# First attention: causal masks added by one full-array bf16 product per head, in place of four over half arrays

## The chip, the cores and the metric

One core of one Trainium2 chip (trn2). The metric is the device time of one execution in microseconds; less is better. The kernel is written in a language that names every instruction, its engine and its semaphores, so nothing is reordered by a compiler: each engine runs its own list in the order in which the source issues it.

## What is computed

The whole is a two-block transformer on x of shape (8, 512, 256): attention with rope, a mixture of 8 experts, a second attention with its MLP, and a mixture of 64 experts. The change touches the first attention only, 16 heads of 16 dimensions over 8 sequences of 512 tokens:

```python
att = jnp.einsum('bhtd,bhsd->bhts', q, k) * (1.0 / math.sqrt(DH))
causal = jnp.tril(jnp.ones((t, t), dtype=bool))
att = jnp.where(causal, att, -jnp.inf)
att = jax.nn.softmax(att, axis=-1)
y = jnp.einsum('bhts,bhsd->bhtd', att, v)
```

## The kernel before

`attention0_phase` works sequence by sequence (8 of them) and, inside one, head pair by head pair (8 pairs, r = 0 to 7). A pair has its two heads j = 0, 1 stacked: head 0 lives in rows (partitions) 0 to 63 of `kq_T`, head 1 in rows 64 to 127. Score products are taken over 64 rows each, the one of head 0 in the upper half of TensorE's array and the one of head 1 in the lower half, and write two different PSUM banks of a ring tile (`banks(k)[:, j, ...]`). q and k carry a high and a low part side by side, which is why 64 rows are used for 16 dimensions.

Each pair is scored twice. The steps a0, a1, a2 (L665 to L679) compute scores with tokens in rows, from which VectorE takes each token's maximum (L468). The maximum is negated and written into the q stack (L474, L477), which step m transposes again (L662). The steps b0, b1, b2 (L681 to L692) compute the transposed scores with the maximum already subtracted, and ScalarE exponentiates them into `probs` (L532). Steps v0 to v3 (L704) multiply them with the values into `pO`, once for two pairs; these products use 32 columns of the array. Step h copies `pO` out on ScalarE (L541), step o transposes it (L712), and VectorE divides (L485, L487). Only blocks on and below the diagonal are computed, one tile of 128 rows by 512, 384, 256 or 128 columns per block row: a0 and b0 hold the one of 512 columns, a1 and b1 those of 384 and 128, a2 and b2 the one of 256. That is 8 tiles per pair, 64 per sequence, 512 in all, and each is done for two heads.

Every tile crosses the diagonal in one 128x128 block, and there the mask is added by TensorE itself, as a product of an identity with a triangle of -1e30 into the same PSUM accumulation. Before the change this product too is taken in halves: the 128 rows of the identity and the triangle are cut into two parts u = 0, 1 of 64 rows, each part is kept twice (in the upper and in the lower half of the partitions), and each head adds both parts from its own half of the array: four products per tile (L676 for a, L690 for b), all in fp32r. Of the two parts one is all zero over half of its columns, so it takes 64 columns and the other 128.

The order of TensorE's work is written out by hand. `STEP` gives the order within a step and how far ahead of the current pair each kind runs, and `BETWEEN` puts the work of neighbouring sequences between: x (transposes of the next sequence's input, L558), p0 to p3 (its qkv projections, L551), t and y (transposes, L577, and projection of the last sequence's attention output). Those, the transposes qk (L656), m and o all use the whole array of 128 rows by 128 columns:

```python
STEP = (("qk", 3), ("a0", 2), ("b0", 0), ("v0", -1), ("m", 1), ("a1", 2), ("b1", 0), ("v1", -1), ("a2", 2),
        ("v2", -1), ("b2", 0), ("v3", -1), ("h", -1), ("o", -1))
BETWEEN = {("qk", 0): ("x",), ("a0", 0): ("p0",), ("a1", 0): ("p1",), ("a0", 1): ("p2",), ("a1", 1): ("p3",),
           ("b1", 0): ("t",), ("b1", 1): ("y",)}
```

v, h and o exist for odd r only. A step with an even pair behind it is called even in this text: it has no v, h, o. The first sequence has no t and y, the last no x and p. Three ring tiles of two PSUM banks go round through qk, a, b, x, p, t and y; a unit may begin when the unit three places earlier has been taken by its reader (`wait_taken`). VectorE and ScalarE run through the same ORDER. GpSimd prepares the next sequence's stacks (L220 to L236).

At the start SP issues the loads one after another on one queue: x of the first sequence, weights, biases and rope, x of the next, then the constants into the unused `probs[2]`, then the third part of x, then stores of zeros to DRAM (L281). VectorE rounds the constants (`constants()`, L377 to L384) between the first bias additions and its share of the first stacks. TensorE's `prepare` ends with waits for the constants, and its first `body` with a wait for the stacks.

Of the kernel before, what the change touches and what calls it, by code (L numbers as in the profile page):

```python
# [24 lines left out]
F32R = mybir.dt.float32r  # L25
BF16 = mybir.dt.bfloat16
# [6 lines left out]
P = 128  # L33
# [55 lines left out]
def attention0_phase(nc, g, t):  # L89

    W3 = 3 * D
    with ExitStack() as ctx:
        def sb(name, shape, dt=F32):
            return ctx.enter_context(nc.sbuf_tensor("a0_" + name, shape, dt))
# [12 lines left out]
        rope = sb("rope", [P, TB, 2, DH0])  # L107
        unrope = sb("unrope", [P, TB, 2, DH0])
        HALF = P // 2
        half_eye = sb("half_eye", [P, 2, P], F32R)  # L110
        mask_ts = sb("mask_ts", [P, 2, P], F32R)
        mask_st = sb("mask_st", [P, 2, P], F32R)
        ident_r = sb("ident_r", [P, P], F32R)

        stats, mv = sb("stats", [P, NT, 6]), sb("mv", [P, NT, 2])
# [25 lines left out]

        w_raw = probs[0][:, :, :].rearrange("p j c -> p (j c)")[:, 0:KC * W3].rearrange("p (c n) -> p c n", c=KC)
        wp_raw = probs[1][:, 0, 0:KC * D].rearrange("p (c n) -> p c n", c=KC)
        const_raw = probs[2][:, 0, 0:6 * P].rearrange("p (m u q) -> p m u q", m=3, u=2)

        ring = [ps(f"ring{k}", (P, 2 * S)) for k in range(3)]
        pT = ps("pT")
# [96 lines left out]
        @block.sync  # L244
        def _(sp):
            x_in = t["x"].rearrange("b (n p) d -> p (b n) d", p=P)

            def load_x(batch):
                a, b = BATCHES[batch]
                sp.dma_start(g.x[:, a:b, :], x_in[:, a:b, :]).then_inc(x_loaded[batch].sem, x_loaded[batch].tick(16))  # L250

            load_x(0)
            for dst, src in (
                (w_raw, t["wqkv"].rearrange("(c p) n -> p c n", p=P)),
                (g.ident[:, :], t["ident"][:, :]),
                (wp_raw, t["wproj"].rearrange("(c p) n -> p c n", p=P)),
            ):
                sp.dma_start(dst, src).then_inc(loaded.sem, loaded.tick(16))
            for dst, src in (
                (bias_qkv[:, :], t["bqkv"].partition_broadcast(P)),  # L260
                (unrope[:, :, :, :], t["unrope"].rearrange("(n p) q d -> p n q d", p=P)),
                (rope[:, :, :, :], t["rope"].rearrange("(n p) q d -> p n q d", p=P)),
                (bias_proj[:, :], t["bproj"].partition_broadcast(P)),
            ):
                sp.dma_start(dst, src).then_inc(rest_loaded.sem, rest_loaded.tick(16))
            load_x(1)
            for j in range(2):
                rows = slice(j * HALF, (j + 1) * HALF)
                for u in range(2):
                    cut = slice(u * HALF, (u + 1) * HALF)  # L270
                    sp.dma_start(const_raw[rows, 0, u, :], t["ident"][cut, :]).then_inc(const_loaded.sem, const_loaded.tick(16))
                    for kind in range(2):
                        sp.dma_start(const_raw[rows, 1 + kind, u, :], t["causal"][kind, cut, :]).then_inc(const_loaded.sem,
                                const_loaded.tick(16))
            load_x(2)

            sp.wait_ge(zeros_ready.sem, zeros_ready.at(1))
            zeros = heads_T[:, :].rearrange("p (n d) -> p n d", d=D)
            step = zeros.shape[1] * P
            for at in range(0, TOKENS, step):  # L280
                sp.dma_start(t["sorted_x"][at:at + step, :].rearrange("(n p) d -> p n d", p=P), zeros).then_inc(zeroed.sem,  # L281
                        zeroed.tick(16))
            sp.wait_ge(zeroed.sem, zeroed.at(zeroed.n))
            for rows, start in (("sorted_x", TOKENS), ("sorted_y", 0)):
                for at in range(start, BLOCKS * SLOT_TOKENS, TOKENS):
                    size = min(TOKENS, BLOCKS * SLOT_TOKENS - at)
                    dst, src = (t[name][a:a + size, :].rearrange("(p r) d -> p (r d)", p=P)
                                for name, a in ((rows, at), ("sorted_x", 0)))
                    sp.dma_start(dst, src).then_inc(spread_zeros.sem, spread_zeros.tick(16))
            sp.wait_ge(spread_zeros.sem, spread_zeros.at(spread_zeros.n))  # L290
# [46 lines left out]
        def _(dve):  # L337
# [38 lines left out]
            def constants():  # L376
                dve.tensor_tensor(wp_lo[:, :, :], wp_raw, wp_hi[:, :, :], ALU.subtract).then_inc(w_split.sem, w_split.tick())  # L377
                assert w_split.n == SPLITS
                dve.tensor_copy(ident_r[:, :], g.ident[:, :]).then_inc(const_split.sem, const_split.tick())
                dve.wait_ge(const_loaded.sem, const_loaded.at(12 * 16))  # L380
                for ins in (
                    dve.tensor_copy(half_eye[:, :, :], const_raw[:, 0]),
                    dve.tensor_copy(mask_ts[:, :, :], const_raw[:, 1]),
                    dve.tensor_copy(mask_st[:, :, :], const_raw[:, 2]),  # L384
                ):
                    ins.then_inc(const_split.sem, const_split.tick())

# [158 lines left out]
        def _(pe):  # L546
# [75 lines left out]
            def body(s, m, before, more):  # L622
                pe.wait_ge(stacked.sem, stacked.at(2 * TB, s))
                absent = (() if before else ("t", "y")) + (() if more else ("x", "p"))
                for what, r in ORDER:
                    if what in absent:
                        continue
                    if (what, r) in PLACE:
                        u = PLACE[what, r]
# [35 lines left out]
                    elif what in ("a0", "a1", "a2"):  # L665
                        pe.wait_ge(evac.sem, evac.at(r + 1, s))
                        for tb, at in A_TILES[int(what[1])]:
                            diag = at + tb * P
                            for j in range(2):
                                rows = slice(j * HALF, (j + 1) * HALF)  # L670
                                pe.matmul(banks(k)[:, j, at:at + (tb + 1) * P], kq_T[rows, q_at(r), tb * P:(tb + 1) * P],
                                          kq_T[rows, k_at(r), 0:(tb + 1) * P], start=True, stop=False)
                            for u, cut in ((0, slice(0, P)), (1, slice(HALF, P))):
                                for j in range(2):
                                    rows = slice(j * HALF, (j + 1) * HALF)
                                    last = pe.matmul(banks(k)[:, j, diag + cut.start:diag + cut.stop], half_eye[rows, u, :],  # L676
                                                     mask_ts[rows, u, cut], start=False, stop=(u == 1))
                        last.then_inc(scores.sem, scores.tick())
                    elif what in ("b0", "b1", "b2"):  # L679
                        if what == "b0":  # L680
                            pe.wait_ge(max_evac.sem, max_evac.at(r + 1, s))  # L681
                        for sblk, at in B_TILES[int(what[1])]:
                            for j in range(2):
                                rows = slice(j * HALF, (j + 1) * HALF)
                                pe.matmul(banks(k)[:, j, at:at + S - sblk * P], kq_T[rows, k_at(r), sblk * P:(sblk + 1) * P],
                                          qT_max[r % 2][rows, sblk * P:S], start=True, stop=False)
                            for u, cut in ((0, slice(0, HALF)), (1, slice(0, P))):
                                for j in range(2):
                                    rows = slice(j * HALF, (j + 1) * HALF)
                                    last = pe.matmul(banks(k)[:, j, at + cut.start:at + cut.stop], half_eye[rows, u, :],  # L690
                                                     mask_st[rows, u, cut], start=False, stop=(u == 1))
                        last.then_inc(shifted.sem, shifted.tick())  # L692
                    elif what in ("v0", "v1", "v2", "v3"):
                        group, sblk = r // 2, int(what[1])
# [1923 lines left out]
```

## Time and profile before

| | |
|---|---|
| median of 3 runs | 2916.57 us (2913.05 to 2918.31) |
| profiled execution, span from first to last instruction | 2917.1 us |
| first attention, from TensorE's first scores to its last | about 54 to 672 us |
| TensorE / VectorE / ScalarE / GpSimd busy over the span | 85% / 63% / 46% / 28% |
| mean granted clock of TensorE | 0.926 |

The page gives no time for the profiled execution beside its span; the span lies within the runs. "PE" is TensorE's products, "PEld" its weight loads, "DVE" VectorE, "ACT" ScalarE, "POOL" GpSimd, "SP" the sync engine. In a product `out<-a,b`, b is the stationary operand that is loaded first. A shape such as 64*128 is the part of the array that is used, rows by columns; 64x384 behind it is what is streamed. Two instructions on the two halves of the array start 2 to 4 ns apart, so the timeline merges them (x2, x4). The end of a product is modelled, so what counts is the distance between starts. The recorded start of a product is never later than the end of its load, but it may be earlier than the time at which it streams.

### The profile page before, as it was taken

What the parts mean: (1) busy time and instruction counts of PE and PEld (TensorE: products, weight loads), DVE (VectorE), ACT (ScalarE), POOL (GpSimd) and SP (SyncE); (2) the same over time, 40 slices, a digit from 0 to 9 for tenths busy, and PEclk for the clock granted to TensorE, in tenths of its full rate; (3) what the DMA queues carried; (4) which work ended last, traced back from release to release, by engine and by line L of the source; (5) the groups of instructions that cost most, each with busy time, mean ns of one, the idle gap of its engine ahead of it and who ended that gap; (6) DMA issues with size and microseconds to landing.
All of it is one profiled execution on the core that took longest, in us unless ns stands there. A gap on an engine that the chain in (4) does not pass through costs nothing. (4 is left out here: it accounts for less than half of the span.)

```text
span 2917.1 us, 54564 instructions
## 1 busy us (share of the span) xinstructions
PE 2480.8 (85%) x20412; PEld 2255.4 (77%) x20412; DVE 1832.5 (63%) x3236; ACT 1348.1 (46%) x2053; POOL 820.9 (28%) x1194
## 2 busy tenths in 40 slices
PE   4888898884279999954688778869999999999999
PEld 3666677773179999953566667759999999999999
DVE  7555555545358888858888888736654544554544
ACT  1454444541156777733334444334445445445454
POOL 6445455503600000024566665530000000000000
PEclk8899999987589999977798889989999999999999
DMA  9992000000367777756555554514422232222222
GB/s 305 338 333 94 1 1 2 1 1 29 114 192 238 227 235 236 233 173 144 135 131 137 137 131 132 132 62 146 128 82 87 78 98 88 86 89 94 81 78 88
DMA packets 194351, 373.36 MB, mean 128 GB/s; under 512 B 28708, under 2 KB 104680, under 8 KB 193128
## 3 DMA queue, kind: packets, MB, share of 16 engines
q1 hardware_dynamic: 184792, 343.31, 38.8%
q0 software_dynamic: 9360, 27.27, 2.7%
q8 instruction: 139, 2.28, 0.3%
q14 instruction: 60, 0.49, 0.1%
HBM read 336.95 MB, written 100.66 MB: 150 GB/s over the span
## 5 line engine op out<-in xcount | busy, mean ns | idle before, releaser
L2325 DVE TENSOR_TENSOR e_h_lo<-e_h,e_h_hi 128x512 fp32r<-128x512 f32 x320 | 221.8, 693 | 300.8 <-ACT e_h_hi L2401 300.8
L2463 PE MATMUL e_h_ps<-e_yT_hi,e_w_hi 128*128 128x256 f32 x1280 | 362.4, 283 | 2.9 <-ACT e_h L2387 2.1
L2479 PE MATMUL e_y_ps<-e_w_hi,e_h_hi 128*128 128x256 f32 x1280 | 358.7, 280 | 2.4 <-DVE e_h_lo L2325 2.2
L2463 PE MATMUL e_h_ps<-e_yT_lo,e_w_hi 128*128 128x256 f32 x1280 | 358.4, 280 | 0.0
L2463 PE MATMUL e_h_ps<-e_yT_hi,e_w_lo 128*128 128x256 f32 x1280 | 358.3, 280 | 0.0
L2479 PE MATMUL e_y_ps<-e_w_hi,e_h_lo 128*128 128x256 f32 x1280 | 355.4, 278 | 0.0
L2479 PE MATMUL e_y_ps<-e_w_lo,e_h_hi 128*128 128x256 f32 x1280 | 355.2, 278 | 0.0
L2401 ACT ACTIVATE e_h_hi<-e_h 128x512 fp32r<-128x512 f32 x320 | 202.2, 632 | 277.1 <-DVE e_h L2320 217.9
L2387 ACT ACTIVATE e_h<-e_h_ps,e_b 128x512 f32<-128x512 f32 x320 | 219.2, 685 | 174.4 <-PE e_h_ps L2463 152.1
L2320 DVE TENSOR_TENSOR e_h<-e_h,e_spread 128x512 f32<-128x512 f32 x256 | 176.7, 690 | 133.7 <-ACT e_h L2387 132.5
L468 DVE TENSOR_REDUCE a_top<-a_ring 128x2 f32<-128x1024 f32 (+3 forms) x256 | 202.8, 819 | 84.6 <-PE a_ring L676 83.7
L2463 PEld LDWEIGHTS e_h_ps<-e_yT_hi,e_w_hi 128*128 128x128 f32 x1280 | 243.6, 190 | 4.7 <-ACT e_h L2387 2.5
L2479 PEld LDWEIGHTS e_y_ps<-e_w_hi,e_h_hi 128*128 128x128 f32 x1280 | 240.9, 188 | 3.9 <-DVE e_h_lo L2325 3.4
L2463 PEld LDWEIGHTS e_h_ps<-e_yT_lo,e_w_hi 128*128 128x128 f32 x1280 | 241.6, 189 | 0.0
L2463 PEld LDWEIGHTS e_h_ps<-e_yT_hi,e_w_lo 128*128 128x128 f32 x1280 | 241.5, 189 | 0.0
L2479 PEld LDWEIGHTS e_y_ps<-e_w_lo,e_h_hi 128*128 128x128 f32 x1280 | 240.7, 188 | 0.2
L2479 PEld LDWEIGHTS e_y_ps<-e_w_hi,e_h_lo 128*128 128x128 f32 x1280 | 240.3, 188 | 0.0
L532 ACT ACTIVATE a_probs<-a_ring 128x1024 f32<-128x1024 f32 (+1 forms) x192 | 167.9, 883 | 133.8 <-PE a_ring L690 132.2
L79 POOL TENSOR_TENSOR e_by_tile<-e_by_tile 128x4 f32<-128x4 f32 x24 | 9.6, 398 | 743.1 <-DVE e_by_tile L71 741.8
L1315 PE MATMUL e_y_ps<-e_w_hi,e_h_hi 128*128 128x256 f32 x624 | 179.0, 287 | 3.7 <-DVE e_h_lo L1205 3.0
L1301 PE MATMUL e_h_ps<-e_xT_hi,e_w_hi 128*128 128x256 f32 x624 | 173.9, 279 | 1.6 <-DVE e_xT_lo L1198 1.6
L1301 PE MATMUL e_h_ps<-e_xT_hi,e_w_lo 128*128 128x256 f32 x624 | 173.6, 278 | 0.0
(364 smaller groups left out, 7033.4 us busy)
## 6 DMA issues: line engine op xcount, KB each, us to landing
e_w<-in_w SPq DMA_DIRECT2D x78, 1024.0 KB, 5.6
e_spread<-share_store SPq DMA_DIRECT2D x512, 128.0 KB, 2.8
a_keys<-rows_store SPq DMA_DIRECT2D x128, 256.0 KB
a_queries<-rows_store SPq DMA_DIRECT2D x86, 256.0 KB, 5.1
a_running_hidden<-rows_store SPq DMA_DIRECT2D x42, 256.0 KB, 4.9
e_xs<-sorted_x SPq DMA_DIRECT2D x39, 256.0 KB, 5.3
sorted_y<-e_ys POOLq DMA_DIRECT2D x39, 256.0 KB, 5.6
e_stage_buf<-in_w_all SPq DMA_DIRECT2D x10, 512.0 KB, 3.6
```

What stands on the lines that cost most here:

```text
L79: pool.tensor_tensor(tmp, guess, guess, ALU.mult).then_inc(step.sem, step.tick())
L468: dve.reduce_max(top[r % 2][:, tb, :], banks(k)[:, :, at:at + (tb + 1) * P], AX.X).then_inc(top_taken.sem, top_taken.tick())
L532: act.activation(probs[r % 3][:, :, B_AT[i]:B_AT[i] + B_WIDTH[i]], banks(k)[:, :, 0:B_WIDTH[i]], ACT.Exp).then_inc(probs_ready.sem, probs_ ...
L1301: last = pe.matmul(h_ps[:, at:at + SLOT_TOKENS], l, r, start=(m == 0), stop=(m == len(ops) - 1))
L1315: last = pe.matmul(y_ps[n][:, 0:D], h_parts[a][:, f, n * P:(n + 1) * P], w2_parts[k][w][:, f, :], start=(f == 0 and m == 0), stop=(f == FC ...
L2320: dve.tensor_tensor(h[:, q % 2, :], h[:, q % 2, :], spread[r % SPREADS][:, :], ALU.mult).then_inc(scaled.sem, scaled.tick())
L2325: dve.tensor_tensor(h_parts[q % 2][1][:, :], h[:, q % 2, :], h_parts[q % 2][0][:, :], ALU.subtract).then_inc(h_lo.sem, h_lo.tick())
L2387: act.activation(h[:, q % 2, :], h_ps[q % 2][:, :], ACT.Silu, bias=b1[:, c:c + 1]).then_inc(h_ready.sem, h_ready.tick())
L2401: act.activation(h_parts[q % 2][0][:, :], h[:, q % 2, :], ACT.Copy).then_inc(h_hi.sem, h_hi.tick())
L2463: last = pe.matmul(h_ps[q % 2][:, cols], l, r, start=(m == 0), stop=(m == len(ops) - 1))
L2479: last = pe.matmul(y_ps[n][:, 0:D], h_parts[q % 2][a][:, n * P:(n + 1) * P], w2[b][:, c, :], start=(q == 0 and m == 0), stop=(q == CH - 1 ...
```

## The change

For the diagonal block, the identity and both triangles are kept once, whole, in bf16 (128 x 128 each). After the two score products of a tile, over 64 rows each, one product over all 128 rows adds the mask for head 0 and a second one for head 1, with 128 columns each: two products per tile in place of four, and none in halves. Each has its own load of the same identity. The constants arrive with 2 loads in place of 12 (the identity is taken from the copy that is loaded anyway).

```diff
-        half_eye = sb("half_eye", [P, 2, P], F32R)
-        mask_ts = sb("mask_ts", [P, 2, P], F32R)
-        mask_st = sb("mask_st", [P, 2, P], F32R)
+        eye = sb("eye", [P, P], BF16)
+        mask_ts = sb("mask_ts", [P, P], BF16)
+        mask_st = sb("mask_st", [P, P], BF16)
...
-        const_raw = probs[2][:, 0, 0:6 * P].rearrange("p (m u q) -> p m u q", m=3, u=2)
+        const_raw = probs[2][:, 0, 0:2 * P].rearrange("p (m q) -> p m q", m=2)
...
             load_x(1)
-            for j in range(2):
-                rows = slice(j * HALF, (j + 1) * HALF)
-                for u in range(2):
-                    cut = slice(u * HALF, (u + 1) * HALF)
-                    sp.dma_start(const_raw[rows, 0, u, :], t["ident"][cut, :]).then_inc(const_loaded.sem, const_loaded.tick(16))
-                    for kind in range(2):
-                        sp.dma_start(const_raw[rows, 1 + kind, u, :], t["causal"][kind, cut, :]).then_inc(const_loaded.sem,
-                                const_loaded.tick(16))
+            for kind in range(2):
+                sp.dma_start(const_raw[:, kind, :], t["causal"][kind, :, :]).then_inc(const_loaded.sem, const_loaded.tick(16))
             load_x(2)
...
-                dve.wait_ge(const_loaded.sem, const_loaded.at(12 * 16))
+                dve.wait_ge(const_loaded.sem, const_loaded.at(2 * 16))
                 for ins in (
-                    dve.tensor_copy(half_eye[:, :, :], const_raw[:, 0]),
-                    dve.tensor_copy(mask_ts[:, :, :], const_raw[:, 1]),
-                    dve.tensor_copy(mask_st[:, :, :], const_raw[:, 2]),
+                    dve.tensor_copy(eye[:, :], g.ident[:, :]),
+                    dve.tensor_copy(mask_ts[:, :], const_raw[:, 0]),
+                    dve.tensor_copy(mask_st[:, :], const_raw[:, 1]),
                 ):
...
-                            for u, cut in ((0, slice(0, P)), (1, slice(HALF, P))):
-                                for j in range(2):
-                                    rows = slice(j * HALF, (j + 1) * HALF)
-                                    last = pe.matmul(banks(k)[:, j, diag + cut.start:diag + cut.stop], half_eye[rows, u, :],
-                                                     mask_ts[rows, u, cut], start=False, stop=(u == 1))
+                            for j in range(2):
+                                last = pe.matmul(banks(k)[:, j, diag:diag + P], eye[:, :], mask_ts[:, :], start=False, stop=True)
...
-                            for u, cut in ((0, slice(0, HALF)), (1, slice(0, P))):
-                                for j in range(2):
-                                    rows = slice(j * HALF, (j + 1) * HALF)
-                                    last = pe.matmul(banks(k)[:, j, at + cut.start:at + cut.stop], half_eye[rows, u, :],
-                                                     mask_st[rows, u, cut], start=False, stop=(u == 1))
+                            for j in range(2):
+                                last = pe.matmul(banks(k)[:, j, at:at + P], eye[:, :], mask_st[:, :], start=False, stop=True)
```

## Rows read from the trace of the kernel before

**Rows 1.** The page, busy time of each engine over the span.

```profile
PE 2480.8 (85%) x20412; PEld 2255.4 (77%) x20412; DVE 1832.5 (63%) x3236; ACT 1348.1 (46%) x2053; POOL 820.9 (28%) x1194
```

**Rows 2.** Table by stretch: a middle sequence, the last; then clock, DMA share, GB/s.

```profile
207.00:284.00 77.00, 67.74 (x744) 52.62 (x733) 42.21 (x77) 37.82 (x49) 38.08 (x56) 1.00 0.41 138
590.00:672.00 82.00, 70.46 (x699) 56.30 (x692) 35.58 (x68) 38.33 (x49) 0.00 (x0) 0.83 0.00 1
```

**Rows 3.** Waits, 54 to 672 us: total, times, longest.

```profile
DVE a_top L468 <- PE a_ring L676: 83.7, 92, 3.1
...
PE a_pT L712 <- ACT a_heads_T L541: 26.5, 32, 0.9
...
PE a_ring L685 <- DVE a_top L468: 6.1, 17, 1.2
```

**Rows 4.** Groups by line, 54 to 672 us: the mask products.

```profile
L690 PE MATMUL a_ring<-a_mask_st,a_half_eye 64*128 64x64 f32 (+1 forms) x1024 | 89.1, 259 | 0.0
L676 PE MATMUL a_ring<-a_mask_ts,a_half_eye 64*128 64x128 f32 (+1 forms) x1024 | 83.9, 246 | 0.0
```

**Rows 5.** Timeline of step a1: start and length in us, engine, line.

```profile
295.44 0.19 PEld L671 LDWEIGHTS a_ring<-a_kq_T 64*128 64x128 f32 x2
...
295.55 0.36 PEld L676 LDWEIGHTS a_ring<-a_mask_ts,a_half_eye 64*128 64x128 f32 x4
...
295.83 0.19 PEld L671 LDWEIGHTS a_ring<-a_kq_T 64*128 64x128 f32 x2
...
295.94 0.30 PEld L676 LDWEIGHTS a_ring<-a_mask_ts,a_half_eye 64*128 64x128 f32 x4
...
296.29 0.19 PEld L551 LDWEIGHTS a_ring<-a_w_hi,a_xnT_hi 128*128 128x128 f32 x1
```

**Rows 6.** Timeline of TensorE's products, from a projection into a half-array tile.

```profile
295.11 0.28 PE L551 MATMUL a_ring<-a_w_lo,a_xnT_hi 128*128 128x256 f32 x1
295.23 0.29 PE L551 MATMUL a_ring<-a_w_hi,a_xnT_lo 128*128 128x256 f32 x1
295.44 0.44 PE L671 MATMUL a_ring<-a_kq_T 64*128 64x384 f32 x2
```

**Rows 7.** Timeline at a border between two full-array steps.

```profile
302.52 0.28 PE L551 MATMUL a_ring<-a_w_hi,a_xnT_lo 128*128 128x256 f32 x1
302.54 0.42 PEld L662 LDWEIGHTS a_pT<-a_ident_r,a_q_stack 128*128 128x128 f32 x4
```

**Rows 8.** Timeline: bf16 loads of the first router.

```profile
772.99 0.29 PEld L1061 LDWEIGHTS r_rank_ps<-r_both,r_ones 128*128 128x128 bf16 x8
```

**Rows 9.** Timeline of step a0 with its 512 columns, and the load behind it.

```profile
299.88 0.19 PEld L671 LDWEIGHTS a_ring<-a_kq_T 64*128 64x128 f32 x2
...
300.45 0.19 PEld L551 LDWEIGHTS a_ring<-a_w_hi,a_xnT_hi 128*128 128x128 f32 x1
```

**Rows 10.** Timeline at the end of a sequence.

```profile
279.49 0.33 PE L690 MATMUL a_ring<-a_mask_st,a_half_eye 64*128 64x64 f32 x4
281.28 0.64 PE L704 MATMUL a_pO<-a_probs,a_v 128*32 128x512 f32 x4 [1.45 <-ACT a_probs L532]
```

**Rows 11.** Timelines of the start: a constant's copy, and TensorE's first wait for stacks.

```profile
33.27 0.81 DVE L383 CAST a_mask_ts<-a_probs 128x256 fp32r<-128x256 f32 x1
...
50.21 0.72 PE L656 MATMUL a_ring<-a_ident_r,a_k_stack 128*128 128x128 f32 x4 [20.26 <-POOL scratch L324]
```

**Rows 12.** Table by stretch: an even step, its a1 to b2, one at half clock, that stretch.

```profile
253.73:258.87 5.14, 4.83 (x63) 4.33 (x62) 3.65 (x7) 4.17 (x5) 0.92 (x2) 1.00 0.00 0
255.26:258.06 2.80, 2.49 (x37) 2.30 (x37) 2.22 (x4) 2.18 (x3) 0.00 (x0) 1.00 0.00 0
78.03:86.80 8.77, 8.45 (x63) 7.51 (x61) 5.17 (x11) 4.16 (x5) 8.54 (x14) 0.50 1.05 353
75.00:91.80 16.80, 16.21 (x113) 12.74 (x109) 10.26 (x20) 7.84 (x9) 16.41 (x26) 0.50 0.98 325
```

**Rows 13.** Timeline of the first sequence: a wait ahead of the lower clock.

```profile
72.17 0.50 PE L685 MATMUL a_ring<-a_qT_max,a_kq_T 64*128 64x512 f32 x2 [1.17 <-DVE a_top L468]
```

## The prediction, made before the changed kernel was run

> **What bounds the kernel now.** I read the page first: TensorE is the busiest engine over the whole span [rows 1]. The change touches only the first attention, so I cut that out with the table by stretch. A sequence takes 77 us there; TensorE is busy 67.7 of them, VectorE 42.2, ScalarE 37.8, at full granted clock [rows 2]. The last sequence, which has no projections of a next one to do, takes longer at a clock of 0.83 in the mean. The waits say the same from the other side: VectorE waits 83.7 us for the mask products of L676 and TensorE only 6.1 us for VectorE's maxima; the larger wait of TensorE, 26.5 us for the head outputs, is a chain that a mask product doesn't touch [rows 3]. So in this phase of 618 us (54 to 672 us) nearly every ns added to or taken from TensorE's stream shows in the time. The mask products are 2048 half-array products [rows 4].
>
> Now the stream itself, in ns by load starts. In tile (1,0)-(2,0) of step a1 the loads start at 295.44 (both halves at once), 295.55, 295.83, 295.94 and then, for the projection behind it, 296.29 [rows 5]. A load holds 0.11 us, it runs while the product before it streams, and the two halves of the array work at the same time. So a short product costs the 0.11 of the next load, not its columns: the 384-column tile takes 0.39 us from its load to the next tile's (0.11 + 0.17 of columns + 0.11), the 128-column tile would take 3 x 0.11 = 0.33 in the middle of a run. What the reader should see next is the step at the end: behind the same last mask product the projection's load comes not 0.11 but about 0.24 later. The product of 64 columns has streamed by 296.19 (last load 296.05, plus 0.11, plus 0.03), and the load starts at 296.29: **0.10 us empty, and then the load's 0.11 with nothing beside it**. The other direction shows it too: 256-column products follow each other every 0.12, but the half-array load that comes behind one starts after 0.21 [rows 6], so 0.09 is lost. Where the border is between two steps of full-array products, no such gap stands: the load starts 0.02 after the last product [rows 7]. The semaphore wait at the border is thus not the cause; the change between products over 64 and over 128 rows is. I take 0.09 us for one change, plus whatever load can't be hidden.
>
> **The change, part by part.** Before, all of a run such as a1, b1 stays in halves, and a change comes only at the run's ends. After, each tile goes half, full, half: two changes per tile.
>
> The eye's load is bf16. The only bf16 loads in the trace are those of the first router, eight in 0.29 us of 0.10 each, so one every 0.027 us [rows 8]. I take 0.03, with 0.11 (the fp32 load) as the upper bound and 0 as the lower. An eye product streams 128 columns: half of the 0.12 for 256, 0.055 to 0.06; two of them, one per head, don't overlap, since both use all rows.
> By the Trainium skill's TensorE: Matmul & The Clock Gate, Back-to-back issue gap, a stream of load and product pairs with 128 columns sustains about 81 ns each; no row here has bf16 pairs of 128 columns. By that the two would cost 0.05 more per tile, and over 512 tiles the sum below would be some 27 us larger.
>
> Tile for a head pair, from its load to the next load:
> - 512, 384 or 256 columns, next step also in halves. Before: 0.11 + columns + 0.11 (0.39 for 384). After: 0.11 + columns + 0.09 + 0.03 + 0.055 + 0.055 + 0.09, for 384 0.60. **+0.21.**
> - 128 columns, next also halves. Before 0.33, after 0.11 + 0.055 + 0.09 + 0.03 + 0.11 + 0.09 = 0.48. **+0.15.**
> - Followed by a full-array step (transposes, projections). Before for 512 columns 0.57 [rows 9]; after, the next load runs beside the second eye product, so 0.11 + 0.23 + 0.09 + 0.03 + 0.055 = 0.51: **-0.06**. For 128 columns before 296.29 - 295.83 = 0.46, after 0.34: **-0.12**. Here the change gains.
> - Followed by the value products, which write 32 columns of the array. I count this as a change as well, as today: +0.09, and +0.03 for 128 columns. If full array to 32-column products costs nothing, it is 0 and -0.06.
>
> Going through ORDER for a middle sequence, the 64 tiles are: 28 of the first kind, 9 of the second, 11 and 4 of the third, 9 and 3 of the fourth. Sum: 28 x 0.21 + 9 x 0.15 - 11 x 0.06 - 4 x 0.12 + 9 x 0.09 + 3 x 0.03 = **+7.0 us a sequence, 56 us for eight**. The first and last sequences lack some of the full-array steps in between, and have stretches at half clock where streams and loads take twice as long: +2.
>
> What of it is covered: the 6.1 us in which TensorE waits for maxima [rows 3] I count as swallowed, as VectorE's work stays as it was. At the end of a sequence ScalarE's exponentials set the pace: the last mask products stand at 279.49, the value products start only at 281.28 [rows 10]. The four tiles ahead of it, +0.6 us, are hidden: -5 over eight. No other wait is near. Behind the slower scores are VectorE's maxima and ScalarE's exponentials; both have over 30 us of slack per sequence, and will only wait longer.
>
> Start-up. SP issues 12 small loads of constants, about 0.6 us each; 2 stay, so the third x load and the zero stores behind them start some 6 us earlier. Nobody waits for those then (the constants are needed at 33 us, the third x load after 60), so 0. If the zero stores did collide with the loads ahead of them, it would be a us. VectorE's three constant copies get half as wide; the two mask copies take 0.81 each, beside a busy GpSimd, and they lie on the path to TensorE's first scores, which wait for the stacked tiles of VectorE (20.3 us) [rows 11]. -0.8 us, between 0 and -1.6.
>
> Sum: 56 + 2 - 6 - 5 - 1 = **+46 us**. On the profiled execution (span 2917.1) this gives 2963; the median of the runs is 0.5 lower, and I say **2962**.
>
> **Rivals.**
> 1. *The eye is loaded ahead and nothing empties* (faster). Every change of shape in the trace stands at the border of two steps, none inside a step, so a load inside one might go ahead under the running products. Then a large tile in a run costs columns + 0.055 + 0.11 against columns + 0.22 (-0.06), a 128 tile -0.11, and the ends of runs gain 0.09 more than above: 28 x -0.06 + 9 x -0.11 + 11 x -0.15 + 4 x -0.21 + 3 x -0.06 = -5.4 a sequence, -43 us, of which ScalarE (4.17 busy in an even step of 5.14 [rows 12]) lets most through: 2880. It decides once the price of an in-step change is below some 0.01 us. Against it: rows 7. Chance 0.06.
> The Trainium skill's TensorE: Matmul & The Clock Gate, Packing small matmuls, gives this mechanism: a load for the background weight buffer or other rows is pulled ahead of running matmuls. By it alone the time would be that 2880; the load of rows 6, held for 0.09 us, doesn't agree.
> 2. *The clock falls* (slower still). At 74.8 us, soon after TensorE had waited 1.17 us at 72.17 and once more behind that [rows 13], the granted clock went to its lower level, 1.2 GHz, and stayed there for 17 us of a and b steps; one such step takes 8.77 us at half against 5.14 at full [rows 12]. The change leaves more empty time in just these steps. If each middle sequence had such a stretch, 17 us in place of 17 x 5.14/8.77 = 10, that is +7 a sequence, some +50 in all: 3012. Against: a1 to b2 of an even step stream 1536 columns of scores and 6 x 192 of masks, 1.12 us at 2.4 GHz of 2.80, or 40%, at full clock [rows 12]; after, 1536 + 6 x 256, 1.28 us of 2 x (0.60 + 0.48 + 0.55) = 3.26, or 39%. Chance 0.20.
> 3. *A change of shape costs more here*, for the wide product before it or the change of type between fp32 and bf16. At 0.10 us more for each of the some 86 changes added per sequence (113 after, 27 before): +69, 3030. Nothing in the trace has fp32 and bf16 products in one stream. Chance 0.14.
> 4. *It vanishes in other waits*: 2917. Speaks for it only that an even step already has ScalarE at 4.17 of 5.14 us; against it the 67.7 against 42.2 [rows 2]. Chance 0.04.
>
> **How the numbers follow.** My forecast has 0.56. Its own range: the change at 0.07 to 0.11, eye loads 0.03 to 0.05, hidden parts 5 to 20 us: 2940 to 2985. To hold 8 in 10 the range must reach rivals 2 and most of 3: 2930 to 3035. Less than about 0.2% (6 us) can't be told from no change. Faster only by rival 1: 0.06. Same: rival 4, 0.04. Slower: 0.90.
>
> **What would show it.** In the profile after: in the a and b steps the load of the eye starts about 0.09 us after the half products have streamed and never beside them; the tile of 384 columns takes 0.60 in a run; a middle sequence takes some 83 us; the idle of VectorE before its maxima and of ScalarE before its exponentials grows by some 20 to 40 us each; the stretches behind 672 us (plus the shift) are as long as before; the granted clock in the middle sequences stays at 0.96 or more. I am wrong if eye loads start beside streaming half products, if the sequences stay at 77 us, or if the clock table shows a new low stretch in them.

## The result and the profile after

The median after is 2950.36 us (2945.12 to 2955.63) against 2915.6 of the kernel before on the same chip: a ratio of 1.0121 [1.0104, 1.0138], **35 us slower**. The profiled execution took 2955.63 us with a span of 2953.9, 36.8 more than the span before, at nearly the same mean clock (0.923 against 0.926); the other executions had spans of 2943.5 to 2949.8 and clocks of 0.926 to 0.927, so this trace is the longest of the four.

The page, busy time by engine; TensorE has 1024 products fewer and is busy 58 us longer [rows 1]:

```profile
PE 2538.3 (86%) x19388; PEld 2200.3 (74%) x19388; DVE 1827.5 (62%) x3236; ACT 1347.8 (46%) x2053; POOL 814.2 (28%) x1194
```

The table by stretch of the kernel after: the first attention, a middle sequence, the last sequence (columns as in [rows 2]):

```profile
54.00:716.00 662.00, 596.03 (x4595) 368.72 (x4593) 339.19 (x649) 298.29 (x379) 265.73 (x401) 0.93 0.28 92
218.70:301.30 82.60, 73.93 (x578) 45.95 (x577) 42.88 (x79) 37.65 (x48) 37.95 (x56) 0.96 0.23 78
636.00:716.00 80.00, 70.59 (x544) 42.01 (x544) 36.14 (x68) 36.94 (x48) 0.00 (x0) 0.89 0.00 1
```

The first attention ends at 715.4 instead of 673.5 us: +41.9, more than the whole loss. Its six middle sequences take 83.1 us in the mean, where they took 76.7 (counted from a sequence's first transposes of stacks to those of the next). VectorE and ScalarE do in one what they did before (42.9 and 37.7 against 42.2 and 37.8): only TensorE's time grew. Behind the phase the trace is 5.1 us shorter than before. The way to the first expert product, through the first router, which nothing of the change touches, takes 134.2 us where it took 142.0, and what follows is 2.8 longer. A second profile of the same kernel (change_again, below) has 142.3 for that way, so I take it for a difference between two executions and not for a gain.

The waits of the first attention, total, times, longest [rows 3]:

```profile
ACT a_probs L526 <- PE a_ring L679: 177.3, 154, 4.5
...
DVE a_top L462 <- PE a_ring L668: 111.4, 117, 3.4
```

ScalarE waits 177.3 us for the shifted scores (132.2 before) and VectorE 111.4 for its scores (83.7 before). Those are the engines that the slower stream feeds. TensorE's own waits hardly count, and its wait for VectorE's maxima went from 6.1 us to one of 1.2:

```profile
PE a_ring L676 <- DVE a_top L462: 1.2, 1, 1.2
```

The weight loads of TensorE, a1 and b1 of one pair, in time (start, duration, engine, line, what is loaded for, how many merged):

```profile
239.60 0.19 PEld L665 LDWEIGHTS a_ring<-a_kq_T 64*128 64x128 f32 x2
239.97 0.11 PEld L668 LDWEIGHTS a_ring<-a_mask_ts,a_eye 128*128 128x128 bf16 x2 [0.19 <-issue]
240.19 0.18 PEld L665 LDWEIGHTS a_ring<-a_kq_T 64*128 64x128 f32 x2
240.45 0.11 PEld L668 LDWEIGHTS a_ring<-a_mask_ts,a_eye 128*128 128x128 bf16 x2
240.66 0.18 PEld L676 LDWEIGHTS a_ring<-a_qT_max,a_kq_T 64*128 64x128 f32 x2
```

This is the case in five lines. A tile of 384 columns reaches from 239.60 to 240.19, 0.59 us, and the one of 128 columns behind it to 240.66, 0.47; before it was 0.39 [rows 5] and 0.33. Fewer loads stand there, but between them are holes. The half products of 384 columns, loaded from 239.60 to 239.71, have streamed by 239.87 (384 / 2.4 GHz = 0.16); the eye's load starts 0.10 later. Over the tiles of full clock, the median from a tile's load to the next load behind its masks is, in us (for the second and third line the difference, without the tiles that end in a wait):

```
next in halves:        512: 0.451 -> 0.647   384: 0.396 -> 0.591   128: 0.334 -> 0.476
next over full array:  512: -0.065   256: -0.073   128: -0.127
next value products:   512, 256: +0.047            128: -0.008
```

At the start VectorE's three copies became narrower, yet TensorE's first transposes of the stacks, with its first scores behind them, came at 50.27 instead of 50.21 [rows 11]. VectorE's timeline there:

```profile
33.02 0.74 DVE L373 CAST a_ident_r<-ident_f 128x128 fp32r<-128x128 f32 x1
33.68 0.76 DVE L376 CAST a_eye<-ident_f 128x128 bf16<-128x128 f32 x1
34.36 0.22 DVE L377 CAST a_mask_ts<-a_probs 128x128 bf16<-128x128 f32 x1
34.49 0.53 DVE L378 CAST a_mask_st<-a_probs 128x128 bf16<-128x128 f32 x1
34.95 0.62 DVE L220 TENSOR_TENSOR a_att<-a_qk,a_unrope 128x128 f32<-128x128 f32 x1
```

The first mask copy is down to 0.22, but the eye takes 0.76 and the other mask 0.53 for half the elements, and the stacks begin at 34.95, 0.22 later than before. The three copies together did become shorter, 1.27 us (33.68 to 34.95) in place of 1.66 (33.07 to 34.73), but they start 0.61 later: the identity's copy ahead of them came only at 33.02, where it had come at 31.86.

### The profile page after: what moved, and what is told of

The parts are those of the page before. It is cut to its first block and busy times, and to the rows that moved or that the text cites. A ratio compares the mean times of both kernels' runs of the same rounds, so it can differ in the third digit from the quotient of the medians.

```text
span 2953.9 us, 52506 instructions
## 1 busy us (share of the span) xinstructions
PE 2538.3 (86%) x19388; PEld 2200.3 (74%) x19388; DVE 1827.5 (62%) x3236; ACT 1347.8 (46%) x2053; POOL 814.2 (28%) x1194
## 5 line engine op out<-in xcount | busy, mean ns | idle before, releaser
L462 DVE TENSOR_REDUCE a_top<-a_ring 128x2 f32<-128x1024 f32 (+3 forms) x256 | 204.5, 820 | 111.8 <-PE a_ring L668 111.4
L526 ACT ACTIVATE a_probs<-a_ring 128x1024 f32<-128x1024 f32 (+1 forms) x192 | 168.5, 882 | 178.4 <-PE a_ring L679 177.3
```

The lines of the kernel that those rows point to most:

```text
L462: dve.reduce_max(top[r % 2][:, tb, :], banks(k)[:, :, at:at + (tb + 1) * P], AX.X).then_inc(top_taken.sem, top_taken.tick())
L526: act.activation(probs[r % 3][:, :, B_AT[i]:B_AT[i] + B_WIDTH[i]], banks(k)[:, :, 0:B_WIDTH[i]], ACT.Exp).then_inc(probs_ready.sem, probs_ ...
```

## The experiments

My theory: TensorE is emptied at each change between products over 64 and over 128 rows, at some 0.1 us each way, and two changes per tile outweigh the shorter mask products. Rivals: mixing fp32 and bf16 in one stream costs it; full-array products and their loads cost it by themselves; the clock costs it. Ratios are to the kernel before, timed on the same chip; differences between kernels are taken from ratios times 2920. The granted clock has two levels, so its mean over an execution tells how long TensorE was at the lower one: twice the span times what the mean lacks to 1. A us there costs some 0.41 us: the same step takes 8.77 us at half clock and 5.14 at full [rows 12], and 1 - 5.14 / 8.77 = 0.41. That is an estimate, from one step.

**halves_bf16**: the kernel before, with bf16 for its cut identity and triangles. Types are mixed, shapes stay.

```diff
-        half_eye = sb("half_eye", [P, 2, P], F32R)
-        mask_ts = sb("mask_ts", [P, 2, P], F32R)
-        mask_st = sb("mask_st", [P, 2, P], F32R)
+        half_eye = sb("half_eye", [P, 2, P], BF16)
+        mask_ts = sb("mask_ts", [P, 2, P], BF16)
+        mask_st = sb("mask_st", [P, 2, P], BF16)
```

> The kernel before with one thing changed: the identity and the two triangles are bf16 in place of fp32r, still in halves, still four products per tile. Theory (a change between 64-row and 128-row products empties the array, about 0.10 us each, and bares the next load): none is added here, and a short product no longer waits for an fp32 load of the mask (0.11 us) but only for a bf16 one, so a tile costs columns + 0.17 in place of columns + 0.22. Up to 0.055 x 512 = 28 us are gained, some of it lost to ScalarE in the even steps: 2890 to 2906. Rival (alternating between bf16 and fp32r products is what costs): as slow as the change or slower, 2940 or more.

Measured: 0.9895 [0.9877, 0.9914], some 30 us faster than before. The loads of its a1:

```profile
227.42 0.19 PEld L671 LDWEIGHTS a_ring<-a_kq_T 64*128 64x128 f32 x2
227.70 0.11 PEld L676 LDWEIGHTS a_ring<-a_mask_ts,a_half_eye 64*128 64x128 bf16 x4
227.78 0.19 PEld L671 LDWEIGHTS a_ring<-a_kq_T 64*128 64x128 f32 x2
227.94 0.11 PEld L676 LDWEIGHTS a_ring<-a_mask_ts,a_half_eye 64*128 64x128 bf16 x4
228.02 0.19 PEld L685 LDWEIGHTS a_ring<-a_qT_max,a_kq_T 64*128 64x128 f32 x2
```

fp32 and bf16 loads alternate with no hole: 0.36 for the 384 tile (0.33 to 0.36 over all at full clock, before 0.396), 0.24 for the 128 tile (0.334). So the change of type costs nothing, and of the two things the change did, bf16 is the one that pays. Not all of the 30 us are loads: the trace has 48 us at the lower clock in the first attention and that before 75, and 27 x 0.41 = 11.

**full_fp32r**: the change with its eye and masks in fp32r instead.

```diff
-        eye = sb("eye", [P, P], BF16)
-        mask_ts = sb("mask_ts", [P, P], BF16)
-        mask_st = sb("mask_st", [P, P], BF16)
+        eye = sb("eye", [P, P], F32R)
+        mask_ts = sb("mask_ts", [P, P], F32R)
+        mask_st = sb("mask_st", [P, P], F32R)
```

> The changed kernel with the identity and triangles in fp32r in place of bf16; whole array, two products per tile. Theory (change of shape): both changes per tile stay, and the loads of the identity cost 0.11 us instead of about 0.02 and 0.066: some 0.12 us more per tile, +50 to +65 us on the changed kernel, 3000 to 3015. Rival (mixing of types): the extra time of the change goes away, 2915 to 2935.

Measured: 1.0741 [1.0697, 1.0785], 181 us slower than the change; I had expected a third of that. Loads and the phase as a whole:

```profile
305.83 0.19 PEld L665 LDWEIGHTS a_ring<-a_kq_T 64*128 64x128 f32 x2
306.21 0.30 PEld L668 LDWEIGHTS a_ring<-a_mask_ts,a_eye 128*128 128x128 f32 x2 [0.19 <-issue]
306.58 0.19 PEld L665 LDWEIGHTS a_ring<-a_kq_T 64*128 64x128 f32 x2
```

```profile
54.00:916.00 862.00, 808.21 (x4592) 540.61 (x4592) 342.28 (x650) 301.19 (x379) 265.41 (x400) 0.74 0.21 70
```

The tile is 0.75 us at full clock, 0.15 more than the change's: each eye load now stands bare for 0.11. That is 77 us for 512 tiles, somewhat over the 50 to 65 that I expected. The rest goes with the clock: 0.74 in the mean over the phase, 0.93 in the change. TensorE ran at the lower level for some 440 us of it, against 92 (sum of the granted-clock readings in the phase). By 0.41 a us that would be 143 us, and with the loads 220, where the two traces lie 199 apart in this phase: the price of half clock is only rough here.

**grouped**: the change, but in a1 and b1 (the diff shows a) the score products of both tiles come first, then the masks of both. Four changes of shape per step become two; the same products are issued (`start` and `stop` now stand once per step and bank).

```diff
-                                          kq_T[rows, k_at(r), 0:(tb + 1) * P], start=True, stop=False)
+                                          kq_T[rows, k_at(r), 0:(tb + 1) * P], start=(at == 0), stop=False)
+                        for tb, at in A_TILES[int(what[1])]:
+                            diag = at + tb * P
                             for j in range(2):
-                                last = pe.matmul(banks(k)[:, j, diag:diag + P], eye[:, :], mask_ts[:, :], start=False, stop=True)
+                                last = pe.matmul(banks(k)[:, j, diag:diag + P], eye[:, :], mask_ts[:, :], start=False,
+                                                 stop=((tb, at) == A_TILES[int(what[1])][-1]))
```

> The changed kernel, but in steps a1 and b1, which hold two tiles, both tiles' half-array score products come first and all four mask products behind them, so that there is one half-full-half round in place of two. Same products, same loads. Theory (change of shape): from the changed kernel's trace a pair of tiles takes 0.588 + 0.476 = 1.06 us; grouped 0.107 + 0.16 + 0.055 + 0.106 + 3 x 0.066 + 0.149 = 0.78, so -0.29 us for each of 128 steps, -37 us, less what other engines' pace swallows: 2913 to 2922. Rival (the full products themselves are the price): 2950, no change.

Measured: 0.9971 [0.9958, 0.9983], 44 us faster than the change.

```profile
236.22 0.30 PEld L665 LDWEIGHTS a_ring<-a_kq_T 64*128 64x128 f32 x4
236.65 0.22 PEld L670 LDWEIGHTS a_ring<-a_mask_ts,a_eye 128*128 128x128 bf16 x4
236.98 0.30 PEld L679 LDWEIGHTS a_ring<-a_qT_max,a_kq_T 64*128 64x128 f32 x4
```

The pair of tiles takes 0.76 in place of the 1.06 above; 0.30 x 128 pairs is 38 us. Nothing was taken out but changes of shape, so full-array products are not dear by themselves.

**full_in_b**, **full_in_a**: the change in the b steps alone, or in the a steps alone; the other keeps its fp32r halves (the diff is full_in_b against the kernel before; full_in_a does the same to the a steps). Both load one array more at the start.

```diff
+        whole = sb("whole", [P, P], BF16)
...
-                            for u, cut in ((0, slice(0, HALF)), (1, slice(0, P))):
-                                for j in range(2):
-                                    rows = slice(j * HALF, (j + 1) * HALF)
-                                    last = pe.matmul(banks(k)[:, j, at + cut.start:at + cut.stop], half_eye[rows, u, :],
-                                                     mask_st[rows, u, cut], start=False, stop=(u == 1))
+                            for j in range(2):
+                                last = pe.matmul(banks(k)[:, j, at:at + P], eye[:, :], whole[:, :], start=False, stop=True)
```

> The kernel before with the change made in the b steps only; the a steps keep their four half products. 256 of the 512 tiles change. Theory: the price is per change of shape, so about half of the +35 us: 2930 to 2938; perhaps a little more, since each a step between two b steps is entered and left anyway. Rival (the clock falls only when both kinds are thin, and makes most of the extra): under 2925.

> The change in the a steps only; the b steps keep their four half products in fp32r. Together with the run that has it in b only (ratio 1.0034, +10 us) it tells whether the parts add up. If they do, a only is +25 us (1.0085). If each is cheap alone because a few waits of other engines take it up, and only both together are dear, a only is about +10 us as well (1.0034), and some 15 us of the whole come from both being there.

Measured: 1.0034 [1.002, 1.0047] and 1.0144 [1.0119, 1.0169], +10 and +42 us where half of the change would be 17. Within the middle sequences both do the same: 80.2 and 80.4 us, +3.5 and +3.7 on 76.7, where the whole change has +5.5 (change_again) and +6.4. Each half thus costs a little more than half of the whole. full_in_a is nevertheless slower than the whole change, since TensorE ran at 1.2 GHz through most of its first sequence:

```profile
74.80:139.70 64.90, 62.47 (x377) 38.73 (x376) 29.91 (x84) 24.41 (x30) 21.47 (x40) 0.50 1.02 333
```

Its first sequence takes 100.0 us, where that of the kernel before takes 81.8. TensorE is busy 62.5 of these 64.9 us, and the clock rose only at 139.7. Why this stretch is 64.9 long, and that of the kernel before 17 at the same place, these runs don't say.

**change_again**: the change unaltered, beside full_in_a and masks_twice.

> The changed kernel itself, unaltered, so that it stands beside the experiments of this call on one chip, and for a second trace. Theory: 1.012 times the kernel before, in the trace some +40 us in the first attention and 0 behind it, give or take 5. Rival (the 5 us that the first trace of it won back behind the first attention are an effect of the change): again less time between the end of the first attention and the first expert product, 134 us in place of 142.

Measured: 1.0121 [1.0106, 1.0137], as before. Its trace ends the first attention at 709.4, +35.9. From there to the first expert product it takes 142.3 us, as before (142.0), so the short way of the first trace was no effect of the change; the rest is 3.4 us shorter (2097.9 against 2101.3), and other traces of this section lie between 2095.6 and 2102.0 there. All of the loss lies in the first attention.

**masks_twice**: the change with each mask product issued twice in a row, in the same shape (-1e30 twice masks the same).

```diff
                             for j in range(2):
+                                pe.matmul(banks(k)[:, j, diag:diag + P], eye[:, :], mask_ts[:, :], start=False, stop=False)
                                 last = pe.matmul(banks(k)[:, j, diag:diag + P], eye[:, :], mask_ts[:, :], start=False, stop=True)
```

> The changed kernel with each mask product issued twice (the sum is then -2e30 where it was -1e30): four full-array bf16 products per tile in place of two, and no further change between half and full. The trace has 0.066 us from one such product to the next, so by the theory, in which a full product costs its columns only, +2 x 0.066 x 512 = +68 us on the changed kernel, less some 5 for waits: 1.033 to 1.036 of the kernel before. Rival (full products cost about half of a tile's extra 0.2 us each): +100 us or more, 1.046.

Measured: 1.0246 [1.0229, 1.0262], 37 us over the change. Little more than half of what I expected. The products follow each other every 0.056 us, so 1024 of them are 57 us, not 68; and the stretches at half clock shrink:

```profile
54.00:746.00 692.00, 630.62 (x5616) 415.14 (x5616) 337.12 (x650) 298.83 (x379) 265.64 (x400) 0.96 0.27 88
```

0.96 in the mean against 0.93, 48 us at the lower level in place of 92 in the first trace and 75 in change_again's. Over all executions the mean clock is 0.932 (median) against 0.924 of change_again on the same chip, that is 42 us less at the lower level: 42 x 0.41 = 17, and 57 - 17 = 40, near the 37 measured. By the two traces alone it would be 27 x 0.41 = 11 and 46. Part of the price of the added products came back through the clock; how much is known only roughly.

**nil_full**, **nil_half**: halves_bf16 with two more products of 8 columns per tile that add zero, at the tile's end. In nil_full they go over all 128 rows, in nil_half over 64 each. Same instruction count and columns; only the shape differs. In the b steps, first nil_full, then nil_half (the a steps alike):

```diff
+                            for j in range(2):
+                                last = pe.matmul(banks(k)[:, j, at:at + 8], half_eye[:, 0, :], nil[:, :], start=False, stop=True)
...
+                            for j in range(2):
+                                rows = slice(j * HALF, (j + 1) * HALF)
+                                last = pe.matmul(banks(k)[:, j, at:at + 8], half_eye[rows, 0, :], nil[rows, :], start=False, stop=True)
```

> The bf16 halves kernel (ratio 0.9895) with two more products per tile behind its masks, each over the full array with 8 columns of zeros, adding nothing. They cost next to no columns (the first router's 8-column products follow each other every 0.026 us), so what they show is the change of shape by itself: into the full array and out again, in a run, 0.10 + 0.01 + 0.05 + 0.10 and the 0.11 of the next score load that is no longer hidden, +0.27 to +0.3 us a tile for 37 tiles of a sequence, some +0.15 and +0.05 for the other 27, about +100 us in all: ratio 1.022 to 1.030, more if the clock falls. Rival (a change costs only where the product behind it is wide or waits for a semaphore): as nil_half, about 1.000.

> As nil_full, with the same number of instructions and columns, but the two zero products run in the two halves of the array, so the shape never changes. Both theories: two short loads and products more at the same time in both halves, 0.03 to 0.06 us a tile, +15 to +30 us on the bf16 halves kernel, ratio 0.995 to 1.000. The difference of nil_full and this one is the price of the change of shape; the theory says 70 us or more, the rival none.

Measured: 1.0263 [1.0241, 1.0285] and 0.9951 [0.9934, 0.9967]. **92 us lie between two kernels that differ in the shape of two products per tile.** The 384 tile of a1, nil_full and then nil_half:

```profile
234.85 0.19 PEld L673 LDWEIGHTS a_ring<-a_kq_T 64*128 64x128 f32 x2
235.13 0.11 PEld L678 LDWEIGHTS a_ring<-a_mask_ts,a_half_eye 64*128 64x128 bf16 x4
235.32 0.11 PEld L681 LDWEIGHTS a_ring<-a_nil,a_half_eye 128*128 128x128 bf16 x2
235.46 0.19 PEld L673 LDWEIGHTS a_ring<-a_kq_T 64*128 64x128 f32 x2
```

```profile
235.19 0.19 PEld L673 LDWEIGHTS a_ring<-a_kq_T 64*128 64x128 f32 x2
235.48 0.12 PEld L678 LDWEIGHTS a_ring<-a_mask_ts,a_half_eye 64*128 64x128 bf16 x4
235.55 0.10 PEld L682 LDWEIGHTS a_ring<-a_nil,a_half_eye 64*128 64x128 bf16 x2
235.58 0.19 PEld L673 LDWEIGHTS a_ring<-a_kq_T 64*128 64x128 f32 x2
```

0.61 against 0.39, both at full clock: two changes are 0.22 dearer than none. Not all of the 92 us are such holes. The mean clock of nil_full is 0.909 and that of nil_half 0.924 (medians of the executions), which makes 104 us more at the lower level, and 104 x 0.41 = 43: nearly half of the 92 comes through the clock. The traces say the same, with 201 us at the lower level in the first attention against 89.

**halves_bf16_b_only**: halves_bf16 without the masks of the a steps. This leaves out the mask of the scores from which the maxima are taken: a token's maximum then runs over later tokens too, and the division takes the difference out again but for rounding.

```diff
-                                pe.matmul(banks(k)[:, j, at:at + (tb + 1) * P], kq_T[rows, q_at(r), tb * P:(tb + 1) * P],
-                                          kq_T[rows, k_at(r), 0:(tb + 1) * P], start=True, stop=False)
-                            for u, cut in ((0, slice(0, P)), (1, slice(HALF, P))):
-                                for j in range(2):
-                                    rows = slice(j * HALF, (j + 1) * HALF)
-                                    last = pe.matmul(banks(k)[:, j, diag + cut.start:diag + cut.stop], half_eye[rows, u, :],
-                                                     mask_ts[rows, u, cut], start=False, stop=(u == 1))
+                                last = pe.matmul(banks(k)[:, j, at:at + (tb + 1) * P], kq_T[rows, q_at(r), tb * P:(tb + 1) * P],
+                                                 kq_T[rows, k_at(r), 0:(tb + 1) * P], start=True, stop=True)
```

> The bf16 halves kernel (ratio 0.9895) without the mask products of the a steps. The maxima are then taken over the diagonal block's later tokens too, which is still an upper bound of each row and cancels in the quotient, so what is computed is the same but for rounding. It asks how much of TensorE's time in the first attention can still be taken out before another engine binds. If TensorE is still the bound: 0.16 us off a large tile of an a step, 0.13 off the small one, 256 tiles, -40 us, ratio 0.976. If ScalarE (4.17 us busy of 5.14 in an even step of the kernel before) and VectorE bind: at most half of it, 0.982 to 0.988.

Measured: 0.9864 [0.9849, 0.9878], the fastest of all, but only 9 us under halves_bf16, for 1024 products less. Its trace has 99 us at the lower clock in the first attention, that of halves_bf16 48: 51 x 0.41 takes back 21 us of a saving that I had put at 40. By the mean clocks of all executions, 0.922 against 0.929, it is 38 us and 16. The other 10 to 15 I can't place; TensorE waits no longer for maxima than it did (7.9 us against 9.9 from 54 to 640 us).

## Why the prediction was right

Forecast +46, measured +35 (36.8 on the profiled spans): sign and mechanism right, size a quarter to a third too large. By its steps:

**The change of shape** was taken at 0.09 us; it measures about 0.10 on the way in (from 239.87 to 239.97 above) and 0.09 back out. nil_full against nil_half and grouped both carry the theory by a time, not only by rows. The Trainium skill's TensorEngine Tiling (Array Packing), Key Properties, says that changing the tiling mode drains TensorE; it gives no price. These runs agree with it: 0.22 us for the two changes at a tile of nil_full, and 92 us in all, the clock's share included.

**The eye's load** failed as a size. I took 0.03 from the router's rows [rows 8] as time with nothing beside it; the second eye load starts 0.015 behind the first (239.972 and 239.987), and the sums close with 0.01 to 0.02. Hence 0.59 and not 0.60 for the 384 tile. In fp32r it is 0.11, which full_fp32r shows.

**The sum per sequence** was +7.0. With the measured medians it is 28 x 0.196 + 9 x 0.142 - 1.26 (next step full-array) + 0.40 (next step values) = **+5.9**, 47 for eight instead of 56. Most of the 9 us are 0.014 per large tile and 0.04 instead of 0.09 in front of the value products: going from full-array to 32-column products costs about half of what I counted.

**What was covered**: the 6.1 us of waits for maxima are swallowed but for 1.2, as said. At the end of a sequence the last mask product stands at 295.13 and the value products at 296.49, behind ScalarE:

```profile
295.13 0.29 PE L679 MATMUL a_ring<-a_mask_st,a_eye 128*128 128x128 bf16 x2
296.49 1.06 PE L692 MATMUL a_pO<-a_probs,a_v 128*32 128x512 f32 x8 [1.07 <-ACT a_probs L526]
```

Before it was 279.49 and 281.28 [rows 10]: the wait shrank by 0.4 us of the 0.6 reckoned, 3.1 over eight (11.6 to 8.5 us). So 4.9 + 3.1 = 8 us were covered and not 11, and 47 - 8 = 39 is what the measured rows give, against +35.9 in change_again and +41.9 in the first trace.

That the total comes out is in part luck, since the parts per sequence don't. In change_again the six middle sequences took 5.5 us more each (6.4 in the first trace), the first one 3.4 and the last nothing (81.3 us from its first transposes to the end of the phase, before 81.7). I had counted the same +7 for all eight, and +2 for half clock on top. The last one's stretch at the lower clock went from 27.3 to 17.1 us, which gives back 4; why its other tiles cost so little stays open. Nor do loads take twice as long at half clock, as the step for the +2 says: in grouped, the 128 tile's load follows that of the 384 tile by 0.165 us at half clock and 0.108 at full.

**The start-up gain** of 0.8 didn't come (+0.06). The three copies took 0.4 less, which their later start used up. By width the two mask copies would have halved; one fell from 0.81 to 0.22, the other only to 0.53, and why isn't shown.

**Rival 2, the clock**, had a chance of 0.20 and came true in a small way. I had said that a new low stretch would show me wrong, and there are five: in the first trace each of the six middle sequences has one 28 to 29 us after its start, where the kernel before has only the first of them (at 160.1). Two of these sequences have a mean clock of 0.92, under the 0.96 that I had named. Of the four low stretches that the kernel before had where one sequence borders on the next, two are left. In change_again four middle sequences have such a stretch. TensorE's timeline and the table of that stretch:

```profile
243.46 0.28 PE L679 MATMUL a_ring<-a_mask_st,a_eye 128*128 128x128 bf16 x2
244.72 0.53 PE L650 MATMUL a_ring<-a_ident_r,a_k_stack 128*128 128x128 f32 x4 [0.98 <-DVE a_xnT_lo L425]
...
246.61 0.36 PE L679 MATMUL a_ring<-a_mask_st,a_eye 128*128 128x128 bf16 x2
246.73 0.73 PE L656 MATMUL a_pT<-a_ident_r,a_q_stack 128*128 128x128 f32 x4
```

```profile
246.70:253.50 6.80, 6.80 (x36) 5.20 (x37) 2.10 (x3) 2.54 (x3) 6.62 (x10) 0.50 0.01 2
```

Two us after a wait of 0.98 us the clock falls, at 246.7, and such products take 0.73 where 0.5 was usual. But a stretch lasts 6.8 us, not the 17 that I priced, and the last sequence's went from 27.3 to 17.1. In all 92 us at the lower level against 75 before: 17 x 0.41 = 7 us in this trace, none in change_again (75), and the other three executions of the result had clocks as high as before (0.926 to 0.927). The clock decides full_fp32r and full_in_a, not this change.

**Rival 1**, that the eye is loaded ahead, is out: no full-array load in these traces starts beside streaming halves; at full clock the soonest comes 0.09 us after they have streamed. **Rival 3**, that it costs more, for the types or for the wide product, is out: the types by halves_bf16, the width by the tiles of 512, 384 and 128 columns, where the change adds 0.196, 0.195 and 0.142, less for the short one only because its masks had cost 0.05 more before. **Rival 4** is out: ScalarE and VectorE wait 45 and 28 us longer for TensorE, whose own waits for them fell by 8 us and no more.

## What to carry to other kernels

Count the borders between shapes on TensorE before counting products: a visit to the full array between half-array products cost some 0.2 us a time, whatever was done there; the four half products, two and two at once, had cost about as much in all as the two full ones do without the changes. Where the larger shape is wanted, put all its products of a step together (grouped: 44 us back, though bf16 masks in halves stay ahead of it, 0.9895 against 0.9971). And take a change apart by its two halves: here bf16 alone, in the old shape, made the kernel 1% faster, and the new shape took that away twice over.

## What the runs showed that was not expected

A 64-row bf16 load holds up the next one for less than an fp32r one: the 384 tile went from 0.396 to between 0.33 and 0.36 in halves_bf16, the 128 tile, which is loads and little else, from 0.334 to 0.241. I hadn't thought of that half of the change as a gain of its own. The price of the fp32 full-array load is hidden in a stream of one shape and stands bare behind a change of shape, and it weighed double there, since TensorE was granted the lower clock for half of the phase: 77 us of loads became 181. Less work can mean a lower clock as well: masks_twice, with 1024 products more than the change, had the higher mean clock (0.932 against 0.924), and halves_bf16_b_only, with 1024 fewer than halves_bf16, the lower one (0.922 against 0.929). What exactly makes the clock fall, no run here separates.
